# Row maxima of two or four heads in one reduce over two PSUM banks, with the causal mask added on TensorE

## The reference

```
xn = layernorm(x)
q, k, v = (xn @ Wq.T + bq), (xn @ Wk.T + bk), (xn @ Wv.T + bv)      # 32 heads of 16
scores = q @ k.T / sqrt(16);  scores = where(causal, scores, -inf)
att = softmax(scores);  out = (att @ v) @ Wo.T + bo
base = xn @ base_W.T + base_b + routed low-rank part
x = x + out + base
```

## Time and profile before

| what | value |
|---|---|
| median of 3 runs | 716.05 us (715.63 to 716.68) |
| span of the profiled execution | 711.7 us |
| time outside the span (median less span) | 4.4 us |
| PE matmuls busy | 635.7 us (89%) |
| DVE busy | 419.8 us (59%) |
| ACT busy | 293.8 us (41%) |
| POOL busy | 86.3 us (12%) |
| mean granted TensorE clock | 0.952 |

### The profile page before, as it was taken

One profiled execution on the slowest core, in us unless ns is written; L12 is line 12 of the kernel. 1 busy time (PEld: TensorE's weight loads), 2 busy tenths in 40 slices (PEclk: granted clock), 3 DMA queues, 4 the chain that ended last, 5 costly groups with the idle time before them and its releaser, 6 DMA issues.

```text
span 711.7 us, 8799 instructions
## 1 busy us (share of the span) xinstructions
PE 635.7 (89%) x3176; PEld 444.5 (62%) x3176; DVE 419.8 (59%) x1139; ACT 293.8 (41%) x498; POOL 86.3 (12%) x107
## 2 busy tenths in 40 slices
PE   3999999999999927983899999999989998999985
PEld 2788888778888715762687865545545555554553
DVE  5676543365532395622497588787878787881003
ACT  4545432243322302121321156656564656477530
POOL 2000000000000086000000350202110201022010
PEclk9999999999999976998799999999998999899998
DMA  6333232011011110469601024515151515111113
GB/s 209 119 113 99 85 118 89 29 60 60 29 60 60 44 45 1 124 204 209 233 29 58 7 46 77 114 42 112 42 113 40 114 42 113 40 32 45 45 29 129
DMA packets 24635, 58.03 MB, mean 82 GB/s; under 512 B 7136, under 2 KB 7648, under 8 KB 24560
## 3 DMA queue, kind: packets, MB, share of 16 engines
q1 hardware_dynamic: 24304, 56.90, 28.9%
q0 software_dynamic: 288, 0.58, 0.4%
HBM read 42.39 MB, written 15.07 MB: 81 GB/s over the span
## 4 chain that ended last, share of the span: by engine, by line
PE 68%; DMA 13%; DVE 9%; ACT 5%; SPq 2%; issue 1%; POOLq 0%; POOL 0%; ACTq 0%; DVEq 0%
PE bank L1088 9%; PE bank L1105 8%; PE slot L1020 8%; PE bank L860 7%; PE slot L860 7%; PE bank L862 7%; PE bank L861 7%; PE slot L861 7%; PE slot L862 7%; DMA u_dram<-u_sb 4%; DMA heads_dram<-attn_lo 4%; DMA den<-u_dram 3%; ACT probs L844 3%; DVE probs L1187 2%; DVE slot L1415 2%
## 5 line engine op out<-in xcount | busy, mean ns | idle before, releaser
L1415 DVE CUSTOM_DVE_ANT_0 slot<-slot,causal 128x512 f32<-128x512 f32 (+3 forms) x384 | 204.4, 584 | 39.6 <-PE slot L1020 37.6
L844 ACT ACTIVATE probs<-bank 128x512 f32<-128x512 f32 (+1 forms) x304 | 155.2, 580 | 96.8 <-PE bank L1088 96.2
L860 PE MATMUL slot<-xt_hi,ring_hi 128*128 128x512 f32 (+2 forms) x248 | 100.0, 403 | 20.5 <-DVE attn_lo L1370 17.0
L1020 PE MATMUL slot<-kst,qst 112*128 112x512 f32 (+3 forms) x288 | 97.1, 364 | 11.5 <-DVE maxcol L1415 8.2
L1088 PE MATMUL bank<-qst,kst 114*128 114x512 f32 (+3 forms) x288 | 98.7, 384 | 4.6 <-ACT probs L844 3.7
L861 PE MATMUL slot<-xt_lo,ring_hi 128*128 128x512 f32 (+2 forms) x248 | 99.0, 399 | 0.0
L862 PE MATMUL slot<-xt_hi,ring_lo 128*128 128x512 f32 (+2 forms) x248 | 98.9, 399 | 0.0
L1088 PEld LDWEIGHTS bank<-qst,kst 114*128 114x128 f32 x288 | 52.0, 192 | 62.3 <-ACT probs L844 51.4
L1105 PE MATMUL bank<-probs,v_sb 128*17 128x512 f32 (+3 forms) x768 | 83.3, 507 | 0.6 <-POOL probs L657 0.6
L1020 PEld LDWEIGHTS slot<-kst,qst 112*128 112x128 f32 x288 | 57.2, 200 | 23.0 <-DVE maxcol L1415 10.7
L860 PEld LDWEIGHTS slot<-xt_hi,ring_hi 128*128 128x128 f32 (+2 forms) x248 | 47.7, 192 | 33.3 <-issue 19.7
(11 more groups left out here) (186 smaller groups left out, 916.8 us busy)
## 6 DMA issues: line engine op xcount, KB each, us to landing
stage<-in_stream SPq DMA_DIRECT2D x43, 512.0 KB, 3.4
heads_dram<-attn_hi SPq DMA_DIRECT2D x8, 512.0 KB
heads_dram<-attn_lo SPq DMA_DIRECT2D x8, 512.0 KB
u_dram<-u_sb SPq DMA_DIRECT2D x16, 256.0 KB, 4.3
qst<-heads_dram SPq DMA_DIRECT2D x12, 256.0 KB, 4.9
kst<-heads_dram SPq DMA_DIRECT2D x12, 256.0 KB, 7.8
stage<-u_dram SPq DMA_DIRECT2D x16, 128.0 KB
stage<-den_dram SPq DMA_DIRECT2D x16, 128.0 KB
```

The lines of the kernel that those rows point to most:

```text
L844: act.activation(probs[:, to:to + heads, 0:n], bank[b % 3][:, 0:heads * n].rearrange("p (h n) -> p h n", n=n), ACT.Exp, scale=HD ** -0.5). ...
L860: pe.matmul(out_ap, a[0], b[0], start=start, stop=False)
L1020: pe.matmul(bank_of(("max", u))[:, 0:n], queries(g, hh % 2)[0:DOT_ROWS, hh // 2, i * P:(i + 1) * P], keys(g)[0:DOT_ROWS, hh // 2, c:c + n] ...
L1415: dve.tensor_tensor_reduce(score, score, causal[:, mask:mask + n], 1.0, -3.0e38, ALU.add, ALU.max, to).then_inc(S["max_free"], 1)
```

## The change

- MAX_UNITS: a unit covers both sides (two adjacent PSUM banks, one of the two slots), and where it is at most 256 keys wide also both heads of a side. It is one head a side or two: 20 units a group in place of 48, with the same 48 score matmuls of the same widths.
- In a unit that touches the diagonal, one matmul for each head, 128 rows by 128 columns in bf16 (`late_row`, an identity, times `late_key`, MASKED above the diagonal), adds the mask into PSUM. That is 32 more matmuls a group, each with its weight load.
- `row_max` is one tensor_reduce over up to 1024 columns, into two or four heads' maxima; the accumulator reads and the bf16 table `causal` are gone. The zero-padded queries stay.
- The rotation is now of two slots of two banks, and "m" takes a slot in it.
- All of group 1 is done within `linear`. Its turn, its negation and its store stand ahead of the loop; on SP `neg_max(1)` stands ahead of the loads of wo0 and wo1.
- MAX_START goes from 6 to 5 and MAX_END from 5 to 4: in the loop the units of group g+1 run from step 5 of group g-1 to step 4 of group g, and the turn is at step 5.

```diff
+def max_units():
+    units = []
+    for i in range(NT):
+        for c in range(0, (i + 1) * P, 512):
+            n = min(512, (i + 1) * P - c)
+            units += [(i, (0, 1), c, n)] if n <= 2 * P else [(i, (0,), c, n), (i, (1,), c, n)]
+    return units
...
-UNIT_COST = 64
-MAX_START = 6
-MAX_END = 5
-EARLY_UNITS = KD * NT
+UNIT_COST = 128
+MAX_START = 5
+MAX_END = 4
...
             neg_max(0)
+            neg_max(1)
             for name in ("wo0", "wo1"):
                 weights(item_at[(name, 0)])
...
+            neg_max_hi(1)
             for g in range(GROUPS):
                 for s, (half, j) in enumerate(QSTEPS):
...
-                pe.matmul(bank_of(("max", u))[:, 0:n], queries(g, hh % 2)[0:DOT_ROWS, hh // 2, i * P:(i + 1) * P],
-                          keys(g)[0:DOT_ROWS, hh // 2, c:c + n], start=True, stop=True).then_inc(S["max_ready"], 1)
+                diagonal = c + n == (i + 1) * P
+                ps = slot_of(("max", u))
+                for side in range(2):
+                    for k, sl in enumerate(slots):
+                        last = pe.matmul(ps[:, side, k * n:(k + 1) * n],
+                                         queries(g, side)[0:DOT_ROWS, sl, i * P:(i + 1) * P],
+                                         keys(g)[0:DOT_ROWS, sl, c:c + n], start=(k == 0),
+                                         stop=(k == len(slots) - 1 and not diagonal), skip_group_check=True)
+                    if diagonal:
+                        for k in range(len(slots)):
+                            last = pe.matmul(ps[:, side, (k + 1) * n - P:(k + 1) * n], late_row[:], late_key[:],
+                                             start=False, stop=(k == len(slots) - 1), skip_group_check=True)
+                last.then_inc(S["max_ready"], 1)
...
-                    if t == 0 and k == 1:
-                        turn_maxima(0)
-                        maxima(UNITS)
-                    if t > 0 or k > 0:
-                        maxima(UNITS + 4 * t + k)
+                    p = max(0, GH * t + k - 2)
+                    for u in range(UNITS * p // (KD * NT - 2), UNITS * (GH * t + k - 1) // (KD * NT - 2)):
+                        maxima(UNITS + u)
...
             for t in range(NT):
                 linear(t)
+            turn_maxima(1)
...
-                score = bank_of(("max", u))[:, 0:n]
-                mask = (NT - 1 - i) * P + c
-                h = 2 * (hh % 2) + hh // 2
-                to = maxcol[:, g % 2, h, i:i + 1] if c == 0 else maxrest[:, g % 2, h, i - NT // 2:i - NT // 2 + 1]
-                dve.tensor_tensor_reduce(score, score, causal[:, mask:mask + n], 1.0, -3.0e38, ALU.add, ALU.max, to
-                                         ).then_inc(S["max_free"], 1)
+                scores = slot_of(("max", u))[:, :, 0:len(slots) * n].rearrange("p b (k n) -> p b k n", n=n)
+                per_head = (maxcol[:, g % 2, :, i] if c == 0 else maxrest[:, g % 2, :, i - NT // 2]
+                            ).rearrange("p (b k) -> p b k", k=2)
+                dve.tensor_reduce(per_head[:, :, slots[0]:slots[-1] + 1], scores, AX.X, ALU.max
+                                  ).then_inc(S["max_free"], 1)
```

More of the change, by code:

```diff
@@ L171 @@
 NPROB = GH * (LAG + 1)
-MAX_UNITS = [(i, hh, c, min(512, (i + 1) * P - c)) for i in range(NT) for hh in range(GH)
-             for c in range(0, (i + 1) * P, 512)]
+def max_units():
[5 more added lines that the diff above has]
+    return units
+MAX_UNITS = max_units()
 UNITS = len(MAX_UNITS)
-UNIT_COST = 64
-MAX_START = 6
-MAX_END = 5
-EARLY_UNITS = KD * NT
+UNIT_COST = 128
+MAX_START = 5
+MAX_END = 4
 VECTOR_COLUMNS = 400
@@ L210, in max_plan @@
     plan = {}
-    for g in range(1, GROUPS):
-        first = 0 if g == 1 else STEPS * (g - 2) + MAX_START + (g == 2)
+    for g in range(2, GROUPS):
+        first = STEPS * (g - 2) + MAX_START
         places = [(p // STEPS, p % STEPS, hh) for p in range(first, STEPS * (g - 1) + MAX_END + 1)
@@ L217, in max_plan @@
                 for q, s, _ in places]
-        n = EARLY_UNITS if g == 1 else 0
-        work = sum(MAX_UNITS[u][3] + UNIT_COST for u in range(n, UNITS))
+        n = 0
+        cost = [2 * len(slots) * w + UNIT_COST for _, slots, _, w in MAX_UNITS]
+        work = sum(cost)
         done = passed = 0
@@ L224, in max_plan @@
                 plan.setdefault(place, []).append(("max", g * UNITS + n, 0))
-                done += MAX_UNITS[n][3] + UNIT_COST
+                done += cost[n]
                 n += 1
@@ L237, in extras @@
     todo = list(MAX_PLAN.get((g, s, hh), []))
-    if g + 1 < GROUPS and (s, hh) == (MAX_END + 1, GH - 1):
+    if 1 <= g < GROUPS - 1 and (s, hh) == (MAX_END + 1, GH - 1):
         todo.append(("m", g + 1, 0))
@@ L258, in psum_users @@
     users += [("a", 0), ("w", 0)]
+    for g in range(2):
+        users += [("max", UNITS * g + u) for u in range(UNITS)] + [("m", g)]
+    users += [(kind, k) for g in range(GROUPS) for s in range(STEPS) for hh in range(GH)
+              for kind, k, _ in extras(g, s, hh) if kind != "o"]
     users = [(user, (2 * (n % 2), 2 * (n % 2) + 1)) for n, user in enumerate(users)]
[L260 to L263, removed]
     return users + [(("o", n), (2 * n, 2 * n + 1)) for n in range(2)]
@@ L281, in build @@
         ident = sb(nodes, "ident", [P, P])
-        causal = sb(nodes, "causal", [P, NT * P], BF16)
+        late_row = sb(nodes, "late_row", [P, P], BF16)
+        late_key = sb(nodes, "late_key", [P, P], BF16)
         x_sb = sb(nodes, "x_sb", [P, NT, D])
@@ L591, in _ @@
                         spread_den(g, 0)
-                    if s == MAX_END + 2 and g + 1 < GROUPS:
+                    if s == MAX_END + 2 and 1 <= g < GROUPS - 1:
                         neg_max(g + 1)
@@ L617, in _ @@
             pool.dma_start(rw_stage[:], router1).then_inc(S["vec_landed"], 16)
[L618 to L621, removed]
+            pool.wait_ge(S["const_ready"], 4)
+            pool.affine_select(out=late_row[:], in_=late_row[:], compare_op=ALU.not_equal, fill=1.0, base=0,
+                               pattern=[[-1, P]], channel_multiplier=1).then_inc(S["const_ready"], 1)
+            pool.affine_select(out=late_key[:], in_=late_key[:], compare_op=ALU.is_ge, fill=MASKED, base=0,
+                               pattern=[[-1, P]], channel_multiplier=1).then_inc(S["const_ready"], 1)
             pool.iota(expert_id[:], pattern=[[1, NE]], base=0, channel_multiplier=0,
@@ L780, in neg_max_hi @@
                     act.wait_ge(S["negm_stored"], 16 * (g - 1))
-                act.activation(negm[:, g % 2, 0, :], bank_of(("m", g))[0:GH * NT, 0:P], ACT.Copy, scale=-1.0
+                act.activation(negm[:, g % 2, 0, :], slot_of(("m", g))[0:GH * NT, 0, 0:P], ACT.Copy, scale=-1.0
                                ).then_inc(S["m_hi"], 1)
@@ L846, in _ @@
                                        ACT.Exp, scale=HD ** -0.5).then_inc(S["exp_done"], 1)
-                    if s == MAX_END + 1 and g + 1 < GROUPS:
+                    if s == MAX_END + 1 and 1 <= g < GROUPS - 1:
                         neg_max_hi(g + 1)
@@ L1015, in maxima @@
                 g = u // UNITS
-                i, hh, c, n = MAX_UNITS[u % UNITS]
+                i, slots, c, n = MAX_UNITS[u % UNITS]
                 wait_slot(pe, ("max", u))
@@ L1361, in _ @@
             turned_lo(7)
-            dve.wait_ge(S["const_ready"], 5)
+            dve.wait_ge(S["const_ready"], 7)
             then(dve.tensor_copy(map_f[:], map_i[:]))
@@ L1452, in _ @@
             neg_max_lo(0)
-            for u in range(UNITS, UNITS + EARLY_UNITS):
+            for u in range(UNITS, 2 * UNITS):
                 row_max(u)
+            neg_max_lo(1)
             dve.wait_ge(S["y_done"], NT)
```

9 lines of the change are left out of this document (6 added, 3 removed).

## The result

The changed kernel takes 739.34 us (737.74 to 742.68, 4 runs) where the kernel before took 715.84 beside it: a ratio of 1.033 (95% interval 1.0296 to 1.0364), 3.3% slower. The profiled execution spans 736.9 us, 25.2 more than before. Slower, and by this much, is what was forecast. But one place cost twice its forecast, and smaller misses the other way made up for it.

A forecast was written before the change was run, and what follows sets the result against it. PE bounds `values` and `linear`; in the loop it stalls in step 6 behind DVE's reciprocal waiting for DMA. Masks +25, moved units +3.6 - 1, start +5.9, stall -10: +23, so 739 us, range 722 to 761.

The forecast's parts named there:

- What bounds the kernel: PE bounds `values` and `linear`; in groups 1 to 5 step 6 stalls behind DVE's reciprocal awaiting DMA, costing 28 us.
- DVE's work hardly less: Row maxima on DVE: a group goes from 24.7 to 22.2 us, off the path everywhere but behind the stall.
- The masks, 25 us: 256 more bf16 matmuls on PE: 3.1 us in `values`, 3.1 in `linear`, 18.6 in the loop.
- The moved units, 3.6 us: Sixteen units of group 1 move from group 0 into `linear`: 3.6 us on PE there, 1 us credited in the loop.
- The start, 5.9 us: Group 0, T being the end of `linear`: late wo loads delay ACT and step 4 by 5.1, lost clock adds 0.8.
- it stays covered: stack(2), issued at about T + 5.7, was to be hidden, as group 2's first maxima come at T + 16.5 or later.
- The stall, -10 us: Groups 1 to 5: PE's wait moves from step 6 to step 5 and costs 3.6 us in place of 5.6.
- The faster case: Rival: PE does not stop at step 5, the stall vanishes and masks are cheap: -5, 711 us; chance 0.11.
- Cheap masks (15 us): Rival: masks on PE cost 15 us in place of 25, the rest as forecast, 729 us; chance 0.18.
- dear ones (52): Rival: changing between fp32 and bf16 on PE makes masks cost 52 us, giving 755 to 765 us; chance 0.13.
- The wo loads: Rival at the loop's start: the loads are hidden anyway, 5.9 us less, 733 us; chance 0.05.
- DVE as the bound in the loop: Rival: with only two slots each second unit waits 0.3 us, adding 15 us over 100 loop units, 754; chance 0.07.

The follow-up runs named there:

- experiment 5: Kernel before, with DVE's reciprocal of the second half's denominators moved behind step 6's row maxima and SP's spreading to step 7: 688.63 us, ratio 0.9643.
- experiment 2: Changed kernel without its 256 mask matmuls: 724.26 us, ratio 1.0153 to the kernel before.
- experiment 6: Changed kernel with DVE's reciprocal behind step 6's row maxima and SP's spreading at step 7: 723.53 us, ratio 1.0126 to the kernel before.
- experiment 9: Changed kernel without its masks and with the reciprocal behind step 6's row maxima: 701.53 us, ratio 0.9845 to the kernel before.
- experiment 1: Changed kernel with SP's loads of wo0 and wo1 back ahead of the store of group 1's maxima: 737.27 us, ratio 1.0351 to the kernel before.
- experiment 8: Changed kernel with later reciprocal, wo loads ahead of group 1's maxima store, masks in one burst a unit, group 2's maxima from step 7: 708.2 us.

## Why the prediction was right, and where it was not

*What bounds the kernel.* Right. PE is full in `values` and `linear`, and the gaps in the loop were the reciprocal's wait for DMA. Moving that one wait took 25 us off the kernel before (experiment 5), 22.0 of them in step 6 where 28 were read; DVE's pace keeps 1.2 us a group there, which I had not put into the 3.7.

*DVE's work hardly less.* The estimate was 1.22 us for 1024 columns; the reduces of 1024 are recorded at 1.225 in the mean, and the group's mean is 1.145. As forecast it moved no time. DVE is 33 us less busy in the page, more than my 8 x 2.5 = 20. The custom reduces with their reads covered 211.9 us, where 8 x 24.7 = 198 were reckoned: in a row they run at 0.65 us each, but one that stands alone is recorded at its full 0.72, and its read of 0.14 comes behind it.

*The masks, 25 us.* Nearly: about 21. The stages give it piece by piece. Without masks `values` takes 2.4 us less and `linear` 3.3 (experiment 2), and a group without a wait takes 2.5 to 2.7 less (experiments 6 and 9): with six such groups 21 us. The totals of experiments 6 and 9 say 20, but with 7 us either way. A lone mask costs the 0.12 us that I took; the term was too large because many masks stand behind short scores or beside a slower engine and cost less. The price that the Trainium skill gives ("TensorE: Matmul & The Clock Gate", "Back-to-back issue gap"), 81 ns, led to an estimated 21 us, which is what the stages add up to. For one mask it is not what the traces show: 0.12 alone, 0.17 for two, 0.07 behind a 128-column score.

*The moved units, 3.6 us.* Right. Experiment 2 tells them from the masks: without masks `linear` takes 37.1 us, 3.4 more than before, and the masks bring the other 3.3. The 1 us credited in the loop can't be read apart. In `values` only 1.6 of 3.1 came, since before PE had stood there 0.87 us for its first maxima and 0.31 at the end, and the masks were 2.4.

*The start, 5.9 us.* This is the step that failed in size: from the end of `linear` to the end of group 0 it is +14.4, where start, masks and credit made 7.2. Up to step 4 the chain was right: SP's store at T + 1.7 (T + 2.0 forecast), the loads at T + 3.7 (T + 4.8), ACT's wait of 4.45 us, and step 4 at T + 14.1 (T + 13.9). What failed is "it stays covered", said of stack(2). That was judged by the time of its issue, which is T + 5.5 as before. PE wanted the stacks at T + 16.8, as forecast, too. But the last of the transfers, issued at T + 8.7, took 10.9 us behind the 1 MB of wo, where it had taken 8.1 before and takes 7.7 in experiment 1, so it landed at T + 19.6. Even before it had landed only 0.1 us ahead of its use (group 2's first maxima stood in step 7, at T + 17.0). PE stood 2.90 us and worked at half clock afterwards. Experiments 1 and 8 show both sides: with the wo loads ahead group 0 is 5 us shorter, and with the later first unit and joined masks another 8.

*The stall, -10 us.* The term for after was near: steps 5 and 6 took 57.2 us, whose work is 41.5 (experiment 6), so 15.7 are stall where 18 were forecast. The term for before was too large: of the 28 us, 22.0 went with the reciprocal (experiment 5), the rest was DVE's pace. Over groups 1 to 5 the reciprocal's wait costs 22.3 us before (178.3 to 156.0) and 15.7 after (182.0 to 166.3). So the stall gives -6.6 and not -10, and all else in these groups +10.3 where 15.5 were forecast; the sum, +3.7 for +5.5, hides two misses. The clock fell in two groups of five, about the half chance that I gave it.

*The sum* was right to 0.3 us by luck: +7 at the start, -1.5 in `values`, -1.8 in the groups, -2.2 ahead and behind, and a difference of the medians 1.7 smaller than that of the spans.

*The rivals.* The faster case needed the stall gone: the change does not do that. Cheap masks (15 us) and dear ones (52) are both off the 21 that the stages give, and the spacing of a lone mask, 0.12, is neither 0.06 nor 0.25. The wo loads were not hidden: ACT waited for them. DVE as the bound in the loop fell with experiment 6.

## What to carry to other kernels

Before you make an engine's work lighter, look for the one instruction ahead of that work which waits for something else: here moving a reciprocal by two steps brought 25 us, and 33 us less work on DVE shortened no stage. A wait that ends with a DMA swallows work that you add ahead of it and gives little back when you remove it, so take the stall out first and price an operation then. Look where the moved wait is felt next: here ACT and PE stood for it at the start of group 7. When a step moves on a queue, follow every transfer behind it to its first user, also those whose issue time does not change.

## What the runs showed of the hardware

The same wait, that of PE in step 5, did or did not cost the clock. In the changed kernel it fell to a mean of 0.75 over steps 5 and 6 in two groups of five, in experiment 1 in three, in experiment 2 in all five; where it fell the pair of steps took 12 to 14 us, where it did not 9.3 to 10.5. The length of the wait alone doesn't tell the cases apart: the clock fell behind waits of 2.3 and 2.4 us and held behind 2.0 and 2.1 in the changed kernel, but fell behind one of 1.5 in experiment 1. In experiment 2 PE had less to do ahead of the wait and waited longer (2.6 to 3.7 us). Once no such wait was left, steps 5 and 6 of experiment 6 repeated to 0.01 us from group to group.

A bf16 matmul of 128 columns in an fp32 stream delays by 0.05 us itself and by 0.07 the fp32 matmul behind it; a second one in the same burst adds 0.05 only. Behind a lone 128-column fp32 matmul it adds 0.07 in all.

One reduce of DVE over two PSUM banks, 1024 columns, takes 1.225 us; two custom reduces of 512 behind each other take 1.30.

The last transfer of a stack, 256 KB, took 8.1 us from issue to landing before, 10.9 behind the two 512 KB loads of wo in the changed kernel, and 7.7 in experiment 1, which issues those loads earlier.
